# Three edits in one launch: attention's rows of maxima moved up and one more key block summed on GpSimd, and the input projection of the scan stage moved from step 3 to step 6

## The reference

```python
scores = jnp.einsum('bhqd,bhkd->bhqk', q, k) * HEAD_DIM ** (-0.5)
attn = jax.nn.softmax(scores, axis=-1)
out = jnp.einsum('bhqk,bhkd->bhqd', attn, v)
...
xz = jnp.einsum('blc,ec->ble', xn, W_in)      # state-space layer
xi, z = jnp.split(xz, 2, axis=-1)
...                                           # causal convolution of xi over 4 positions, silu -> xc
dbl = jnp.einsum('bld,ed->ble', xc, W_x)      # gives dt, B, C; delta = softplus(dt @ W_dt.T + b_dt)
def step(hst, xs):
    d_t, B_t, C_t, u_t = xs
    dA = jnp.exp(d_t[:, :, None] * A)
    hst = hst * dA + (d_t * u_t)[:, :, None] * B_t[:, None, :]
    return (hst, jnp.einsum('bdn,bn->bd', hst, C_t))
```

## Time and profile before

| | us |
|---|---|
| median of 3 runs | 3976.04 (3971.3 to 3979.86) |
| profiled execution | 3973.87 |
| its span in the trace | 3972.2 |
| attention, first to last exponential | 104.6 to 2115 |
| feed-forward, convolutions, whitening | about 2115 to 2680 |
| state-space layer | about 2680 to 3972 |

### The profile page before, as it was taken

One profiled execution on the slowest core, in us unless ns is written; L12 is line 12 of the kernel. 1 busy time (PEld: TensorE's weight loads), 2 busy tenths in 40 slices (PEclk: granted clock), 3 DMA queues, 4 the chain that ended last, 5 costly groups with the idle time before them and its releaser, 6 DMA issues. The chain is left out here.

```text
span 3972.2 us, 56517 instructions
## 1 busy us (share of the span) xinstructions
PE 3373.5 (85%) x19062; PEld 1207.9 (30%) x19062; DVE 2573.4 (65%) x3346; ACT 2001.1 (50%) x2381; POOL 1924.1 (48%) x620
## 2 busy tenths in 40 slices
PE   6999999999999999999995999657777777777777
PEld 2333333333333333333331333422222222222222
DVE  5677677676676776767750222237777777777777
ACT  3566566565565665656652333234454445444554
POOL 0555566555565655556653000016555655555555
PEclk7899999999999999999997999778888888888888
DMA  2000000000000000000003210134323332333242
GB/s 95 12 14 15 10 17 15 15 15 10 15 17 15 9 15 15 15 15 12 15 9 92 90 63 16 56 103 146 136 96 139 115 130 96 139 115 128 96 143 102
DMA packets 74768, 235.22 MB, mean 59 GB/s; under 512 B 13089, under 2 KB 14181, under 8 KB 74421
## 3 DMA queue, kind: packets, MB, share of 16 engines
q1 hardware_dynamic: 69460, 215.06, 16.0%
q0 software_dynamic: 5056, 16.83, 1.2%
HBM read 192.42 MB, written 39.39 MB: 58 GB/s over the span
## 5 line engine op out<-in xcount | busy, mean ns | idle before, releaser
L526 DVE TENSOR_REDUCE at_pmax<-at_ring 128x1 f32<-128x512 f32 x2048 | 1305.1, 685 | 512.5 <-PE at_ring L334 511.6
L479 ACT ACTIVATE at_probs<-at_sc 128x1024 f32<-128x1024 f32 x1024 | 992.5, 1021 | 660.4 <-PE at_sc L401 660.3
L580 POOL TENSOR_TENSOR at_prob_sums<-at_prob_sums,at_probs 128x2048 f32<-128x2048 f32 x192 | 869.3, 4527 | 109.7 <-ACT at_probs L479 98.7
L398 PE MATMUL at_sc<-at_QT,at_KT 32*128 32x512 f32 x4096 | 847.8, 642 | 21.9 <-issue 21.6
L1634 POOL TENSOR_TENSOR ss_drive<-ss_du,ss_bsb 128x1024 f32<-128x1024 f32 x261 | 610.0, 2350 | 424.9 <-DVE ss_state L1591 417.8
L580 POOL TENSOR_TENSOR at_prob_sums<-at_probs 128x2048 f32<-128x2048 f32 x64 | 291.0, 4547 | 791.2 <-ACT at_probs L479 791.2
L410 PE MATMUL at_O<-at_probs,at_V 128*32 128x512 f32 x4096 | 539.2, 610 | 53.0 <-DVE at_att L549 51.8
L1534 ACT ACTIVATE ss_decay<-ss_delta,ss_a 128x512 f32<-128x512 f32 x520 | 353.2, 687 | 441.8 <-DVE ss_state L1587 304.0
L1423 PE MATMUL ss_Y<-ss_seen,ss_ident 128*128 128x512 f32 x1032 | 540.1, 649 | 0.0
L1599 DVE TENSOR_TENSOR ss_seen<-ss_state,ss_C 128x1024 f32<-128x1024 f32 x259 | 316.3, 1221 | 256.4 <-PE ss_C L1411 249.8
L334 PE MATMUL at_ring<-at_KH,at_QH 32*128 32x512 bf16 x2048 | 447.4, 389 | 5.7 <-DVE at_pmax L526 2.9
(11 more groups left out here) (199 smaller groups left out, 2728.2 us busy)
## 6 DMA issues: line engine op xcount, KB each, us to landing
ss_bsb<-scratch_rows SPq DMA_DIRECT2D x265, 512.0 KB, 6.8
scratch_attn<-at_att SPq DMA_DIRECT2D x64, 256.0 KB, 2.0
fc_att<-scratch_attn SPq DMA_DIRECT2D x32, 512.0 KB, 5.8
ss_xn<-scratch_xm SPq DMA_DIRECT2D x34, 256.0 KB, 5.5
at_xn<-scratch_xn SPq DMA_DIRECT2D x32, 256.0 KB, 3.8
ss_xw<-scratch_xw SPq DMA_DIRECT2D x17, 256.0 KB, 3.7
ln_x<-in_x SPq DMA_DIRECT2D x8, 512.0 KB, 4.4
scratch_xn<-ln_xn POOLq DMA_DIRECT2D x8, 512.0 KB, 3.0
```

Source lines behind the costliest of these rows:

```text
L398: nc.tensor.matmul(sc[:, h, :], KT[head(h), par, blk(kb)], QT[head(h), par, hs(half)], start=True, stop=False)
L479: nc.scalar.activation(probs[:, kb, two, :].rearrange("p h q -> p (h q)"), sc[:, two, :].rearrange("p h q -> p (h q)"), ACT.Exp, scale=SCA ...
L526: nc.vector.tensor_reduce(pmax[:, quad // 2, h, quad % 2:quad % 2 + 1], ring[:, unit[3], :], AX_X, ALU.max, negate=True).then_inc(max_done, 1)
L580: nc.gpsimd.tensor_tensor(prob_sums[:, half, :, :], before, probs[:, k, :, :], ALU.add).then_inc(pool_sums, 1)
```

## The change

It has three parts. GpSimd makes five additions over six key blocks for each half and not four over five, and PE then sums two blocks and the total and not three. The two row matmuls of heads 0 and 1 are issued ahead of the score matmuls of heads 2 and 3. And `AT_X` goes from 3 to 6, `AT_CONV` too.

```diff
-    SUMMED = 4
+    SUMMED = 5
@@ scores()
                     nc.tensor.matmul(sc[:, h, :], KT[head(h), par, blk(kb)], QT[head(h), par, hs(half)], start=True, stop=False)
-                for h in range(GH):
-                    row = slice(h * DH, h * DH + 1)
-                    m = nc.tensor.matmul(sc[:, h, :], ones_bf[row, :], nrow[row, half, :], start=False, stop=True)
                     if h % 2:
+                        for of in (h - 1, h):
+                            row = slice(of * DH, of * DH + 1)
+                            m = nc.tensor.matmul(sc[:, of, :], ones_bf[row, :], nrow[row, half, :], start=False, stop=True)
                         m.then_inc(sc_ready, 1)
@@ state_space_phase()
-        AT_X, AT_CONV, AT_Z, AT_BC, AT_REST, AT_MID, AT_DT, AT_LOW, AT_DELTA = 3, 4, 8, 9, 10, 11, 12, 12, 13
+        AT_X, AT_CONV, AT_Z, AT_BC, AT_REST, AT_MID, AT_DT, AT_LOW, AT_DELTA = 6, 6, 8, 9, 10, 11, 12, 12, 13
```

## The result

The changed kernel takes 3701.84 us (median of 4 runs, 3700.42 to 3704.22), against 3974.7 us for the kernel before (3971.3 to 3979.86, 4 runs). The ratio is 0.9313, with a 95% interval of 0.9297 to 0.9329. The forecast was 3725: the gain was 273 us where 251 had been forecast. The span of the profiled execution is 3698.7 us.

A forecast was written before the change was run, and what follows sets the result against it. Attention was bound by a loop of ACT and PE (3.18 us a blocked step), the state-space layer by DVE, waiting for C behind a late transfer. 3973.87 − 57 − 59 − 154 + 19 = 3723, so 3725 us; eight in ten: 3690 to 3795.

The forecast's parts named there:

- Denominators: Attention, PE: one source less, 0.89 us each, in 64 halves gives 57 us; GpSimd's sums keep some 4.7 us of margin.
- step 9: Attention, row order: the step becomes free, 0.68 us, but 0.27 is lost to a bank DVE reads, leaving 0.41 a group.
- Order of the rows: Attention: earlier `sc_ready` makes plain steps alternate between 2.49 and 3.19 us, saving 1.84 a group, 59 us in 32 groups.
- step 15: Attention, row order: this step saves 0.69 us a group.
- steps 5 and 13: Attention, row order: each of these two steps saves 0.37 us a group.
- the first rival: Attention: the row order brings nothing, because DVE or the ring of banks binds first; 3784 us, chance 0.11.
- Step 0: Attention, row order: the step hangs on chains through ACT and DVE that don't change, so its gain is 0.
- Projection: State-space layer: moved to step 6, all 15 waits go, about 10.3 us each, 154 us, less 19 for the low clock.
- The 19 for meetings with the low clock: State-space layer: a quarter of the images run the projection at low clock, costing 19 us, bounds 3 and 75.
- The second rival: State-space layer: the projection meets the low clock in every image; 3781 us, chance 0.10.
- the third: Attention, strict starting order: scores 2 and 3 start with rows 0 and 1, 5.1 us a group lost; 3947 us, chance 0.05.
- the fourth: Attention: changes between 32-row scores and one-row matmuls empty the array, 10.5 us a group lost; 4121 us, slower, chance 0.02.

## Why the prediction was right, and where its sizes were off

*Denominators (57).* Right in mechanism and size. A source is worth 0.86 to 0.87 on PE, for 0.89 in the forecast, 1.73 a group, 55 us. GpSimd's margin was given as 4.7 on average, and is 3.8 in step 9 and 5.3 in step 1 (L385 at 885.73, the sum at 862.09 + 18.34 = 880.43).

*Order of the rows (59).* The mechanism was right: completion follows the program and starting the array rows. The size was 1.57 a group, 50 us, where 1.84 had been forecast. Term by term, from the starts of scores in the kernel with this part alone (medians over the groups): step 15 gave 0.68 (forecast 0.69), step 9 0.34 (0.41), and steps 5 and 13 gave 0.11 each, where 0.37 had been forecast. This is the term that failed. I had taken the bank of the ring into account in step 9 alone, but "turn" takes a bank in steps 4 and 12, so that the last maximum of step 4 has to wait for the reduction of head 1's. The timelines of DVE and PE after show it:

```profile
839.31 1.29 DVE L526 TENSOR_REDUCE at_pmax<-at_ring 128x1 f32<-128x512 f32 x2 [0.47 <-PE at_ring L334]
```

```profile
840.49 0.55 PE L334 MATMUL at_ring<-at_KH,at_QH 32*128 32x512 bf16 x2
840.75 1.24 PE L398 MATMUL at_sc<-at_QT,at_KT 32*128 32x512 f32 x8
841.71 0.50 PE L402 MATMUL at_sc<-at_nrow,at_ones_bf 1*128 1x512 bf16 x4
```

The reduction ends at 839.31 + 1.29 = 840.60, the second of the two maxima follows (0.55 for the pair and not 0.39), and all scores of step 5 stand behind it until 840.75, 0.26 after t0. That is the 0.37 − 0.11. It is the first rival's mechanism in two steps of sixteen. Step 0 gave 0.29, which I had put at zero, as hanging on a chain that doesn't change. Its last maximum needs the bank of the "q" projection, which is free when DVE has cast `at_QH`. Before, ACT took that projection, behind its exponentials, 1.74 us after its start (922.47, 924.21), and the cast ended at 924.85 + 0.69 = 925.54; the scores started at 925.68, 0.27 behind the first of the two maxima (925.41). With the rows moved ACT takes it 1.16 after its start (900.20, 901.36), and maxima and scores start together (903.14).

*Projection (154 − 19).* The 154 was right: all 15 stalls are gone, at 10.3 each. The 19 for meetings with the low clock was wrong: nothing was lost there. In the changed kernel the projection costs DVE nothing in any image, and with the stalls went the low clock in step 8: its interval fell by 1.23 in the mean, against 0.42 and 0.53 more in steps 9 and 12 and 0.16 in step 1. That is a net of 0.1 an image, 2 us in all, so what the change gained from the clock lay nearly all in the stall itself, in the 6.22 that became 3.60. DVE's wait for C is 79.8 and not the 115 of the forecast. I had read the low clock in step 8 as plain running. The counts above show that it went with the stall, in 6 to 15 of 16 images in kernels with one, and in 2 at most without.

*The second rival* is refuted by the same rows, *the third* by the scores at 840.75, which all start ahead of the rows (841.71), and *the fourth* by rows at 838.15 and scores at 838.42, less apart than the 0.39 that rows take. The Trainium skill ("TensorE: Matmul & The Clock Gate", "The mechanism") would have matmuls start in program order. The trace decides against it: the scores of heads 2 and 3 start with the others at 840.75, ahead of the rows of heads 0 and 1 at 841.71, and in the kernel with one maximum ahead that maximum starts at 844.64, behind all the scores that stand after it. As far as completion goes, the trace agrees: ACT starts 0.43 and not 0.93 us after the rows that it needs.

*Chances.* The forecast's own range was 3695 to 3755, and the time lies in it, near its lower end: 23 us below the centre. The projection brought 24 more than forecast (159 for 135), the rows 9 less and the denominators 2 less. Some 5 us more were gained in the attention outside the plain groups and 4 in the rest of the program, which no term of mine covers. There is some luck in the time lying within that range: the misses have both signs, 33 us one way and 11 the other, and the 33 alone would have led to 3692.

## What to carry to other kernels

Completion signals come in program order even where matmuls run side by side, so put whatever releases another engine ahead of work that starts late. But put nothing there whose own semaphore isn't up yet: that holds everything behind it, as the maximum of head 1 did, for 267 us in all. When a wait on PE goes, price the low clock too, right behind the wait first (6.22 us for 3.60 in a stall), and then in the other steps: that was 36 us between the projection in step 4 and in step 6, and only 2 between steps 3 and 6. And when two small gains meet at one engine (GpSimd here), check its margin before adding them.

## What the hardware showed that I had not expected

- A matmul that waits for busy array rows is passed by later ones on other rows, and one that waits for a semaphore is not: plain steps of 2.83 us on average with head 0's maximum ahead of the other scores, and 3.53 with head 1's there too, which waits for its bank.
- With the projection in step 4, a stall for a transfer is followed by a second stretch at the low clock four steps later in nearly every image (0.59 at 3093 to 3099, for a wait that ended at 3072), with the clock at 1.00 between the two (3079 to 3086).
- Waits of 1.61 and 1.62 us, in the same place of two groups, were followed by a clock of 1.00 in one and of 0.69 in the other.
